# The causal mask of the score maxima: from VectorE's reduction to a matmul on TensorE

## What is computed

```python
att = jnp.einsum('bhqd,bhkd->bhqk', q, k) / np.sqrt(HEAD_DIM).astype(np.float32)
causal = jnp.tril(jnp.ones((T, T), dtype=bool))
att = jnp.where(causal, att, 0.0)
att = jax.nn.softmax(att, axis=-1)
out = jnp.einsum('bhqk,bhkd->bhqd', att, v)
```

## Time and profile before

| | |
|---|---|
| median of 3 runs | 1269.22 us |
| lowest, highest | 1269.14, 1276.57 us |
| the profiled execution: time | 1269.22 us |
| its span (first to last instruction) | 1267.5 us |
| its mean granted TensorE clock | 0.969 |
| token stage, about | 0 to 270 us of the span |
| one middle group of four heads, without the loop's end | about 120 us |

### The profile page before, as it was taken

The page is one execution under the profiler, slowest core; times in us unless marked ns, Lnnn a source line. Parts: engine busy times, 40 slices in busy tenths (PEclk is TensorE's granted clock), DMA queues, the critical chain, the costliest instruction groups (busy, mean ns, idle before and its releaser), DMA issues.

```text
span 1267.5 us, 26802 instructions
## 1 busy us (share of the span) xinstructions
PE 1134.8 (90%) x7168; PEld 470.0 (37%) x7168; DVE 962.7 (76%) x2433; ACT 743.7 (59%) x1553; POOL 361.1 (28%) x716
## 2 busy tenths in 40 slices
PE   2999388879998989998979999999899999999998
PEld 1666154533333323332333333333333333333345
DVE  5777388768689958895879689968696898689722
ACT  1554233236765766576647766676467667666773
POOL 6122011333314231323132313242223232314221
PEclk9999799979999989998989999999799999899999
DMA  2454953305400820091008200900090018002033
GB/s 91 140 176 144 152 186 116 99 19 69 75 5 6 96 49 6 6 104 42 5 8 96 51 4 7 142 7 3 6 122 27 2 25 124 6 2 76 6 97 112
DMA packets 59130, 79.57 MB, mean 63 GB/s; under 512 B 6112, under 2 KB 48480, under 8 KB 57952
## 3 DMA queue, kind: packets, MB, share of 16 engines
q1 hardware_dynamic: 57824, 73.56, 29.6%
q0 software_dynamic: 1152, 4.19, 1.1%
HBM read 43.78 MB, written 29.36 MB: 58 GB/s over the span
## 4 chain that ended last, share of the span: by engine, by line
PE 54%; issue 11%; DVE 9%; ACT 1%; POOL 1%; DVEq 1%; POOLq 0%; DMA 0%; SPq 0%; ACTq 0%
PE ps_o L1065 17%; PE ps_s L1051 16%; PE ps_m L210 15%; DVE part_max L225 3%; PE ps_o L1075 2%; PE ps_m L1097 2%; DVE ps_m L221 2%; ACT probs L933 1%; DVE row_max L238 1%; DVE part_max L221 1%; POOL after L202 1%; PE ps_x L1042 1%; PE ps_x L1043 1%; DVE turned L968 1%; PE ps_x L1028 1%
## 5 line engine op out<-in xcount | busy, mean ns | idle before, releaser
L933 ACT ACTIVATE probs<-ps_s 128x512 f32<-128x512 f32 (+3 forms) x1280 | 610.2, 535 | 309.1 <-PE ps_s L1051 304.4
L225 DVE TENSOR_REDUCE part_max<-ps_m 128x1 f32<-128x512 f32 x730 | 474.3, 681 | 37.8 <-PE ps_m L210 36.3
L1051 PE MATMUL ps_s<-q_op,k_op 99*128 99x512 bf16 (+3 forms) x1280 | 434.2, 358 | 16.8 <-issue 7.7
L210 PE MATMUL ps_m<-k_op,q_op 96*128 96x512 bf16 (+3 forms) x1200 | 405.3, 357 | 34.2 <-DVE part_max L225 24.4
L221 DVE CUSTOM_DVE_ANT_0 ps_m<-ps_m,mask 128x384 f32<-128x384 f32 x470 | 229.7, 497 | 136.4 <-PE ps_m L210 134.2
L1065 PE MATMUL ps_o<-probs,v_sb 128*32 128x512 f32 (+3 forms) x2560 | 306.0, 551 | 8.3 <-POOL probs L881 8.2
L881 POOL TENSOR_SCALAR_AFFINE_SELECT probs<-probs 128x128 f32<-128x128 f32 x512 | 143.2, 296 | 409.3 <-ACT probs L933 402.5
L1051 PEld LDWEIGHTS ps_s<-q_op,k_op 99*128 99x128 bf16 x1280 | 122.3, 98 | 337.3 <-ACT probs L933 222.1
L210 PEld LDWEIGHTS ps_m<-k_op,q_op 96*128 96x128 bf16 x1200 | 118.3, 99 | 191.6 <-DVE part_max L225 86.3
L848 POOL TENSOR_TENSOR diag_weight<-ident,masked_weight 128x2048 f32<-128x2048 f32 x32 | 115.5, 3610 | 123.8 <-ACT masked_weight L900 123.8
L1065 PEld LDWEIGHTS ps_o<-probs,v_sb 128*32 128x32 f32 x2560 | 51.1, 109 | 98.7 <-issue 41.7
(11 more groups left out here) (84 smaller groups left out, 869.2 us busy)
## 6 DMA issues: line engine op xcount, KB each, us to landing
parts_d<-parts SPq DMA_DIRECT2D x48, 256.0 KB, 3.0
q_op<-parts_d SPq DMA_DIRECT2D x48, 256.0 KB, 14.9
k_op<-parts_d SPq DMA_DIRECT2D x48, 256.0 KB, 16.5
vpad_d<-v_pad SPq DMA_DIRECT2D x32, 256.0 KB, 3.2
v_sb<-vpad_d SPq DMA_DIRECT2D x8, 1024.0 KB, 26.6
x_in<-x SPq DMA_DIRECT2D x8, 512.0 KB, 4.9
ffn_d<-ffn SPq DMA_DIRECT2D x8, 512.0 KB, 3.2
attn_t<-normed SPq DMA_DIRECT2D x128, 32.0 KB, 2.3
```

What stands on the lines that cost most here:

```text
L210: last = pe.matmul(ps_m[:, f % ring, 0:width], self.q_op[0:ROWS, p, h, q0:q0 + P], self.k_op[0:ROWS, p, h, pc * CH:pc * CH + width], start ...
L225: dve.tensor_reduce(self.part_max[:, u % 2, h * SUB + s, pc:pc + 1], ps_m[:, f % ring, 0:width], AX_X, ALU.max).then_inc(self.piece_reduce ...
L933: act.activation(probs[:, slot % PRING, 0:width], ps_s[:, slot % SRING, 0:width], ACT.Exp).then_inc(probs_ready, 1)
L1051: pe.matmul(ps_s[:, slot % SRING, 0:CH - q0], k_op[0:KROWS, p, h, kt * P:(kt + 1) * P], q_op[0:KROWS, p, h, u * CH + q0:(u + 1) * CH], sta ...
```

## The change

The mask becomes a 128 x 128 matrix, `mask16`, and is added by TensorE: behind the score matmul of a diagonal piece, a second matmul, with the bf16 identity as its weights and `mask16` streamed through, accumulates the mask onto the last 128 columns of the piece in PSUM. The score matmul's accumulation then stays open (`stop=(pc < u)`), and `piece_ready` is incremented by the mask matmul. VectorE reduces every piece with `tensor_reduce`, whose width is 128 to 512; the masking reduction, its write back to PSUM and the increment of `diagonal_seen` are gone.

```diff
--- before.py
+++ after.py
@@ -141,7 +141,7 @@
         self.v_after = sb("v_after", [P, 2, NT, GH * HW])
         self.keys_after = sb("keys_after", [P, P])
         self.ones = sb("ones", [P, P])
-        self.mask16 = sb("mask16", [P, CH], BF16)
+        self.mask16 = sb("mask16", [P, P], BF16)
         self.floor = sb("floor", [P, GH, NT])
         self.part_max = sb("part_max", [P, 2, GH * SUB, NCH])
         self.raw_max = sb("raw_max", [P, GH, SUB])
@@ -155,7 +155,6 @@
         self.v_loaded = [sem("v_loaded0"), sem("v_loaded1")]
 
         self.piece_ready, self.piece_reduced = sem("piece_ready"), sem("piece_reduced")
-        self.diagonal_seen = sem("diagonal_seen")
         self.raw_ready, self.max_ready = sem("raw_ready"), sem("max_ready")
         self.hi_ready, self.rest_ready = sem("shift_hi_ready"), sem("shift_rest_ready")
         self.mid_ready, self.shift_ready = sem("shift_mid_ready"), sem("shift_ready")
@@ -174,7 +173,7 @@
 
         pool.affine_select(out=self.keys_after[:], in_=self.ones[:], compare_op=ALU.is_gt, fill=0.0, base=0,
                            pattern=[[-1, P]], channel_multiplier=1).then_inc(self.consts_made, 1)
-        pool.affine_select(out=self.mask16[:, CH - P:CH], in_=self.mask16[:, CH - P:CH], compare_op=ALU.is_ge, fill=NEG, base=0,
+        pool.affine_select(out=self.mask16[:], in_=self.mask16[:], compare_op=ALU.is_ge, fill=NEG, base=0,
                            pattern=[[-1, P]], channel_multiplier=1).then_inc(self.consts_made, 1)
         pool.affine_select(out=self.floor[:, :, NT - 1], in_=self.floor[:, :, NT - 1], compare_op=ALU.not_equal, fill=LOWEST,
                            base=-(P - 1), pattern=[[0, GH]], channel_multiplier=1).then_inc(self.consts_made, 1)
@@ -208,20 +207,16 @@
         pe.wait_ge(self.piece_reduced, base + (f + 1 + MRING - ring if f else MRING))
         q0 = u * CH + s * P
         last = pe.matmul(ps_m[:, f % ring, 0:width], self.q_op[0:ROWS, p, h, q0:q0 + P],
-                         self.k_op[0:ROWS, p, h, pc * CH:pc * CH + width], start=True, stop=True)
+                         self.k_op[0:ROWS, p, h, pc * CH:pc * CH + width], start=True, stop=(pc < u))
+        if pc == u:
+
+            last = pe.matmul(ps_m[:, f % ring, s * P:width], self.ident16[:], self.mask16[:], start=False, stop=True)
         last.then_inc(self.piece_ready, 1)
 
     def reduce_piece(self, dve, ps_m, ring, f, base):
 
         u, h, s, pc, width = piece(f)
         dve.wait_ge(self.piece_ready, base + f + 1)
-        if pc == u:
-
-            dve.sem_inc(self.diagonal_seen, 1)
-            dve.tensor_tensor_reduce(ps_m[:, f % ring, 0:width], ps_m[:, f % ring, 0:width],
-                                     self.mask16[:, CH - width:CH], 1.0, LOWEST, ALU.add, ALU.max,
-                                     self.part_max[:, u % 2, h * SUB + s, pc:pc + 1]).then_inc(self.piece_reduced, 1)
-            return
         dve.tensor_reduce(self.part_max[:, u % 2, h * SUB + s, pc:pc + 1], ps_m[:, f % ring, 0:width], AX_X,
                           ALU.max).then_inc(self.piece_reduced, 1)
```

## The result

The changed kernel takes 1272.9 us (median of 20 runs, 1261.8 to 1282.0) against 1268.3 us before (20 runs, 1256.9 to 1276.6). The ratio is 1.0052 with an interval of 1.0027 to 1.0079: half a per cent slower, 3 to 10 us, less than the runs of one kernel differ among themselves. The ratio is taken from the fast runs (one of the 20 after counts as slow); the two medians alone give 1.0037. The forecast was 1280 us, range 1264 to 1298, with "within 1%" the likeliest of the three outcomes. Direction and outcome came out and the time lies in the range; the size is about half of the forecast (5 to 7 us for 11). Two of the terms behind it were far too small, as the experiments show.

What follows compares the result with a forecast made beforehand. The prediction took TensorE, busy 90%, as the main bound, with VectorE setting the pace in some stretches. From 1269.22 us, masks +13.4, VectorE's pace -2, round trip -1.4 and token stage +1 gave +11.0: 1280 us, range 1264 to 1298.

Steps and rivals of the forecast that it cites:

- Part 1: VectorE's diagonal pieces: the accumulator read delays nothing, a plain reduction spares 0.012 us a piece, -2 us.
- The "about 200" pieces: Diagonal pieces of the attention stage, of 470, where VectorE sets the pace and the sparing counts: -2 us.
- Part 2: Diagonal pieces' round trip, mostly in a group's last unit: 0.1 to 0.15 us shorter, 0.2 us a group, -1.4 us.
- one of its rivals: Faster case: reads hold up VectorE; matmul rows overlap, so waits exceed recorded idle; -20 us, 1249, chance 0.08.
- Part 3: Mask matmuls on TensorE: 0.057 us each, partly hidden in idle time, 1.85 us a group exposed, 13.4 us together.
- the 2.4 us in question: Token stage: 42 masks cost at most 2.4 us, or nothing if filled into waits; taken as +1.
- The clock: TensorE's half-speed stretches in the attention stage may move or become fewer: every case wider by some 7 us; no chance given.
- the full price everywhere: Rival: all 512 masks on TensorE cost their full distance, 29 us, 1298; chance 0.22.
- "Faster" by the read: Rival: the accumulator read holds up VectorE, each diagonal piece gains 0.14 us; -20 us, 1249; chance 0.08.
- The "no change" rival: Shorter round trip removes the last unit's waits, idle time there takes all 25 masks: +4 us, 1273; chance 0.25.

Runs made afterwards that it cites:

- no_mask: The changed kernel without the mask matmul, later keys of the diagonal block left in the maximum: 1259.7 us, 0.9925 of before.
- no_mask_again: The changed kernel without the mask matmul, run again in the second set: 1259.9 us, 0.9940 of before.
- The increments: The changed kernel with semaphore increments between VectorE's wait and a diagonal piece's reduction: one 1276.7 us, two 1286.6 us; one before every reduction 1284.2 us.
- mask_added: The kernel before with the mask matmul added on TensorE and VectorE's masking reduction kept: 1282.6 us, 1.0081 of before.
- the fill: The changed kernel without the mask matmul, plus 12 unused matmuls a group in unit 2's piece-free stretch: 1257.0 us, 0.9920 of before.

## Why the prediction was right, and where it was not

**Part 1, right in its mechanism.** The accumulator read does not set VectorE's pace: VectorE's busy time fell by 12.5 us and not by 80, the stretch that VectorE paces did not get shorter (7.98 us from its first score matmul to its last in the clean groups of both kernels), and no_mask stayed above 1248. The 0.012 us a piece is borne out (0.01). The "about 200" pieces for which it was counted are not worked out: the one stretch that VectorE paces has 2 diagonal pieces a group.

**Part 2, the step that failed.** Its durations were right: 0.09 us sooner where 0.1 was worked out, net of the mask. Its price was not: "I take 0.2 us a group" and bounds of -1.0. VectorE's part of the change, pace and round trip together, is worth 13.4 to 14.3 us at equal clock, where the sum had 2 + 1.4. It came from reading no idle time in the earlier trace rows as no wait: in the stretch where TensorE was busy 26.10 of 26.10 us, no_mask is 0.4 us shorter with the same work on TensorE. Matmul by matmul, the whole difference lies ahead of five pieces, none with a recorded idle time. One of them, before and in no_mask_again:

```profile
870.97 0.34 PE L210 MATMUL ps_m<-k_op,q_op 96*128 96x384 bf16 x1
871.14 0.38 PE L1051 MATMUL ps_s<-q_op,k_op 99*128 99x512 bf16 x1
871.51 0.39 PE L210 MATMUL ps_m<-k_op,q_op 96*128 96x512 bf16 x1
```

```profile
1113.86 0.33 PE L209 MATMUL ps_m<-k_op,q_op 96*128 96x384 bf16 x1
1114.02 0.38 PE L1043 MATMUL ps_s<-q_op,k_op 99*128 99x512 bf16 x1
1114.26 0.39 PE L209 MATMUL ps_m<-k_op,q_op 96*128 96x512 bf16 x1
```

The last piece starts 0.37 us behind the score matmul before, 0.24 us without the mask. A matmul's row (0.38 us) ends 0.16 us after the next could have started (0.22), so waits shorter than that don't show as idle. The prediction said this in one of its rivals and did not use it in its own sum. The increments then measured the price: 5 to 7 us for each 0.1 us on the diagonal pieces. By that rate, as an estimate, the 0.15 us sooner start against mask_added, with 0.06 us of earlier release, is 11 to 14 us. What is left for the pace is little: 0.01 us on each of 470 pieces would be 5 us at the very most. How the 14 us divide between start, release and pace beyond the increment's 5.2 was not measured apart.

**Part 3, the distance right, the cover wrong.** The median distance from one of the 512 masks to the next start is 0.058 us. Where a float32 matmul (`ps_o`) follows it is 0.149, but so it is behind a 128-column piece without a mask. Stretch by stretch, the shortest clean length among the six middle groups in each kernel (from score matmul to score matmul, us; no_mask from both of its runs; the predicted exposure beside it):

| stretch | masks | before | no_mask | after | masks' cost | predicted |
|---|---|---|---|---|---|---|
| unit 0 | 6 | 10.61 | 10.41 | 10.64 | 0.23 | 0 |
| unit 1, first 2 tiles | 2 | 7.98 | 7.97 | 7.98 | 0.01 | 0 |
| unit 1, rest | 6 | 16.33 | 15.88 | 16.19 | 0.31 | 0.21 |
| unit 2, with pieces | 8 | 22.95 | 22.74 | 23.09 | 0.35 | 0.21 |
| last unit, tiles 0 to 2 | 15 | 9.30 | 8.99 | 9.74 | 0.75 | 0.46 |
| tiles 3 and 4 | 5 | 7.50 | 7.20 | 7.33 | 0.13 | 0 |
| tiles 5 to 12 | 17 | 26.14 | 25.69 | 26.67 | 0.98 | 0.97 |
| tiles 13 to 15 | 5 | 9.04 | 8.87 | 8.99 | 0.12 | 0 |
| sum | 64 | | | | 2.88 | 1.85 |

The stretch paced by VectorE hides its masks, the one paced by TensorE pays in full, as said; against the kernel before it grew by 0.53 alone, since the shorter round trip gives back 0.45 there. In between, idle time does not take up masks one for one: a mask delays what comes behind it even where TensorE waits later, and the round trip that had made the waits is shorter. Seven groups and the last one make 21 us. What the 42 masks of the token stage cost can't be read: its end moved from 271.3 to 273.5 us (271.1 and 270.5 without masks), but with two masks it is 270.5 and with one mask and an increment 275.5, so it differs more from run to run than the 2.4 us in question. In all 21.5 us at equal clock for 13.4 + 1.

**The clock, called a widening that changes no sign.** It is a term of the sum. The mean clock was 0.962 to 0.964 without masks, 0.966 before, 0.970 after, so that the change gets back some 4 us against before (0.0035, at 1.2 us for each 0.001). The traces, one execution each, point the same way: from the piece-free end of unit 2 to tile 2 of the last unit, the half-clock time of all groups adds up to 34.1 and 23.9 us without masks, 20.5 before, 3.4 after and 0 with the fill. With it go TensorE's waits for GpSimd in the piece-free stretch: 15.1 and 10.5, 8.2, 4.8 and 1.2 us. Before, the clock fell behind the waits of 2.31, 1.81 and 1.62 us and not behind those of 1.08 and 1.10. That wait is a term that the prediction did not have at all; in these kernels it was shorter, as a rule, the longer the work ahead of it took. Clock and wait were not measured apart.

The sum as measured: +21.5 (masks) - 13.5 (VectorE) = +8, less some 4 for the clock: +4, in the interval of 3 to 10. The split is rougher than the total: by the clean stretches the first two are +21 and -16, +5.5 together, and the runs after come from outside the two sets. The sum as predicted: +11. Two terms were too small by 7 and by 10 us with opposite signs, and the clock took some 4: that the total came out better than its parts is luck.

Of the rivals, the full price everywhere falls: 21 us for the first mask and 20 for the second, of 29. "Faster" by the read falls too. The "no change" rival had the mechanism that was undervalued, the shorter round trip, and its 1273 is what was measured; but the 25 masks that it hides in the last unit cost 1.00 us a group by the table, so its number is luck as well.

**A better kernel.** A row's maximum serves only to keep the exponentials in range; a maximum that includes some later keys of the diagonal block is an upper bound, and the result is the same. no_mask, which simply drops the mask of the maxima, takes 0.9925 and 0.9940 of the time before in two sets, and with the fill 0.9920. It beats both kernels by 8 to 16 us. It would not do for inputs where a masked score exceeds a row's real maximum by so much that the exponentials vanish in float32.

## What to carry to other kernels

Matmul rows overlap, so an engine that is "busy 100%" can still be waiting in steps shorter than the overlap; compare distances of starts, and price a round trip through a ring of buffers by adding a known delay to it. A small op moved to the busiest engine costs its full distance of starts wherever that engine sets the pace, and where it doesn't, idle time need not take it up. And before moving a mask, ask whether the value it protects needs it.

## What was not expected of the hardware

- A semaphore increment between VectorE's wait and its op delays the op's start by 0.11 us, and a second one by another 0.09 us (medians of 30 to 33 waits, 128-column pieces).
- More matmuls need not cost time: with 96 added ones, put where TensorE waited for GpSimd, the mean granted clock was 0.972 in place of 0.964, and the time did not rise.
- Runs of one kernel lie up to 20 us apart (4 to 20, by kernel). A line through the granted clock, at 1.0 to 1.5 us for each 0.001, leaves 1 to 2 us of it unexplained in all kernels but the filled one.
